# A graph attention loop on one core: operands of long VectorE instructions moved to PSUM, and one matmul in place of two

## The reference, cut to what matters

```
for t in range(3):
    xw = x @ W[t];  a_s = xw @ att_src[t];  a_d = xw @ att_dst[t]
    e_raw  = leaky_relu(a_s[src] + a_d[dst], 0.2)
    m      = maximum(segment_max(where(edge_type == t, e_raw, -inf), dst), e_self)
    w_edge = where(edge_type == t, exp(e_raw - m[dst]), 0)
    num    = segment_sum(w_edge[:, None] * xw[src], dst) + w_self[:, None] * xw
    denom  = segment_sum(w_edge, dst) + w_self
    out   += num / denom[:, None] + bias[t]
```

## Time and profile before

| | us |
|---|---|
| median of 3 timed runs | 4762.41 |
| lowest and highest of them | 4758.4, 4772.9 |
| span of the profiled execution | 4747.3 |
| TensorE busy in it | 4230.1 (89%) |
| VectorE busy in it | 2606.6 (55%) |
| ScalarE busy in it | 1243.8 (26%) |
| POOL busy in it | 3328.1 (70%) |

### The profile page before, as it was taken

One profiled execution on the slowest core, in us unless ns is written; L12 is line 12 of the kernel. 1 busy time (PEld: TensorE's weight loads), 2 busy tenths in 40 slices (PEclk: granted clock), 3 DMA queues, 4 the chain that ended last, 5 costly groups with the idle time before them and its releaser, 6 DMA issues. The chain is left out here.

```text
span 4747.3 us, 64017 instructions
## 1 busy us (share of the span) xinstructions
PE 4230.1 (89%) x18574; PEld 3279.7 (69%) x18575; DVE 2606.6 (55%) x6278; ACT 1243.8 (26%) x3966; POOL 3328.1 (70%) x3261
## 2 busy tenths in 40 slices
PE   7899999999999999999977888888989988898988
PEld 5677777777777777777755667776767766676776
DVE  6777777777777777777755222233322332333233
ACT  4433333333333333333322111111111111111111
POOL 3777777777777777777712777777777777777774
PEclk9655566666666666666657666666566566656567
DMA  2222222222222222222233222222222222222223
GB/s 80 50 50 47 48 48 48 48 48 48 48 48 48 48 48 48 48 48 48 48 70 97 72 70 70 70 72 70 70 71 70 71 70 71 69 71 70 70 70 73
DMA packets 215746, 288.25 MB, mean 61 GB/s; under 512 B 136193, under 2 KB 143929, under 8 KB 215722
## 3 DMA queue, kind: packets, MB, share of 16 engines
q0 software_dynamic: 105472, 222.39, 20.0%
q1 hardware_dynamic: 110250, 65.57, 5.0%
HBM read 277.81 MB, written 9.81 MB: 61 GB/s over the span
## 5 line engine op out<-in xcount | busy, mean ns | idle before, releaser
L54 POOL DMA_INDIRECT ae_xg<-table,ae_idx x1620 | 1675.0, 1034 | 639.7 <-issue 464.0
L54 POOL DMA_INDIRECT ce_xg<-table,ce_idx x1620 | 1623.2, 1002 | 499.9 <-issue 493.6
L1041 DVE TENSOR_TENSOR ce_msg<-ce_ps_f,ce_fb 128x768 f32<-128x768 f32 x270 | 258.6, 958 | 1359.9 <-PE ce_ps_f L995 1359.9
L1014 PE MATMUL ce_ps_h<-ce_ea,ce_fw 50*128 50x384 f32 x1080 | 664.2, 757 | 248.5 <-DMA ce_ea<-in_edge_attr 246.8
L995 PEld LDWEIGHTS ce_ps_f<-ce_fw,ce_hid 128*128 128x128 f32 x3240 | 657.7, 307 | 247.6 <-issue 247.6
L551 PE MATMUL ae_ps_a<-ae_e,ae_xg 128*128 128x96 f32 x3240 | 768.9, 401 | 64.4 <-DVE ae_e L662 64.4
L551 PEld LDWEIGHTS ae_ps_a<-ae_e,ae_xg 128*128 128x128 f32 x3240 | 648.8, 292 | 165.2 <-DVE ae_e L662 89.7
L975 ACT ACTIVATE ce_hid<-ce_ps_h,ce_fb 128x768 f32<-128x768 f32 x270 | 243.3, 901 | 1871.2 <-PE ce_ps_h L1014 1871.2
L995 PE MATMUL ce_ps_f<-ce_fw,ce_hid 128*128 128x128 f32 x3240 | 733.1, 411 | 0.0
L512 ACT ACTIVATE ae_e<-ae_e,ae_sc 128x96 f32<-128x96 f32 x1620 | 459.7, 362 | 955.3 <-DVE ae_e L654 955.3
L1004 PEld LDWEIGHTS ce_ps_a<-ce_hot,ce_msg 128*128 128x128 f32 x3240 | 591.7, 278 | 0.0
(11 more groups left out here) (141 smaller groups left out, 3634.1 us busy)
## 6 DMA issues: line engine op xcount, KB each, us to landing
ce_ea<-in_edge_attr SPq DMA_DIRECT2D x270, 150.0 KB
ae_xg<-table,ae_idx POOLq DMA_INDIRECT x1620, 2.6
ce_xg<-table,ce_idx POOLq DMA_INDIRECT x1620, 2.6
fa_inv_den<-rden SPq DMA_DIRECT2D x7, 1344.0 KB, 7.5
ae_idx<-in_src SPq DMA_DIRECT2D x276, 3.0 KB
...
```

Of the source, the lines that this page charges most:

```text
L54: eng.indirect_dma_start(out=out, out_offset=None, in_=table[:, :], in_offset=bass.IndirectOffsetOnAxis(ap=idx, axis=0)).then_inc(done, 16)
L1014: last = nc.tensor.matmul(ps_h[:, k * 512:k * 512 + H], fw1[:, :], ea[:, s % XS, k * H:(k + 1) * H], start=True, stop=True)
L1041: nc.vector.tensor_tensor(msg[:, s % 3, :, :], ps_f[s % 2][:, 0:CH * D].rearrange("p (c f) -> p c f", c=CH), fb2[:, :].unsqueeze(1).to_bro ...
```

## The change

All of it is in the attention loop.

- `iota` (0 to 95) is copied once into a PSUM bank, `ps_held`, and `off` reads it there. A new part of `look_up`, `hold`, copies the unit's scores (128x6) into the same bank, and `mask` reads them there.
- ScalarE writes the exponentials into two PSUM banks, `ps_e`, not double buffered, three chunks in each; `weights` reads them there and writes the SBUF tile as before, as two instructions of 288 columns instead of one of 576. `off` stays in SBUF.
- For that banks are shared anew: the transpose and `ps_z` share one, and the rise (now `fall`), the denominators and the sums of a unit share `ps_a`. The exponential of the rise stays in PSUM, in place, and `scale_sums` and `scale_denominators` read it there. Since the sums are written to the same bank, both are moved ahead of `weights`.
- The constant matrix has SLOPE in row 0 and -1 in row 32. One matmul over 64 rows of the state takes SLOPE * a_d minus the maximum straight from it, in place of L568 and L579. It waits for `s_max`, since it reads the maximum that the fourth part of `raise_max` writes, and stands behind the matmul of the fall.

```
+    c[0, 2 * P:3 * P] = SLOPE
     c[32, 2 * P:3 * P] = -1
...
+        ps_tz, ps_held = pb("ps_tz"), pb("ps_held")
+        ps_c, ps_a, ps_e = ([pb(f"ps_{k}{b}") for b in range(2)] for k in "cae")
...
-                        nc.scalar.activation(by_chunk[b][:, c, :], by_chunk[b][:, c, :], ACT.Exp, bias=sc2[:, b, c:c + 1])
+                        nc.scalar.activation(ps_e[c // 3][:, c % 3 * KEYS:(c % 3 + 1) * KEYS], by_chunk[b][:, c, :], ACT.Exp, bias=sc2[:, b, c:c + 1])
...
-                    nc.scalar.activation(rescale[:, b, :], ps_d[b][:, KEYS:2 * KEYS], ACT.Exp).then_inc(s_e, 1)
+                    nc.scalar.activation(ps_a[b][:, 2 * KEYS:3 * KEYS], ps_a[b][:, 2 * KEYS:3 * KEYS], ACT.Exp).then_inc(s_e, 1)
...
-                        nc.tensor.matmul(kv(ps_c[b][:, KEYS:2 * KEYS]), h.slope[0:1, :], state[0:1, :, bass.ds(base[s], W)], start=True, stop=False).then_inc(s_dst, 1)
...
                         pe.wait_ge(s_rise, n)
-                        nc.tensor.matmul(ps_c[b][:, KEYS:2 * KEYS], h.less_row32[0:64, :], rise[:, 0, :], start=False, stop=True).then_inc(s_c, 1)
-                        nc.tensor.matmul(ps_d[b][:, KEYS:2 * KEYS], h.less_row32[0:64, :], rise[:, 1, :], start=True, stop=True).then_inc(s_fall, 1)
+                        pe.wait_ge(s_max, n)
+                        nc.tensor.matmul(ps_a[b][:, 2 * KEYS:3 * KEYS], h.lower[0:64, :], fall[:, :], start=True, stop=True).then_inc(s_fall, 1)
+                        nc.tensor.matmul(kv(ps_c[b][:, KEYS:2 * KEYS]), h.lower[0:64, :], state[0:64, :, bass.ds(base[s], W)], start=True, stop=True).then_inc(s_c, 1)
...
-                        nc.vector.tensor_tensor(off[:, s % 3, :, :], h.iota.unsqueeze(1).to_broadcast([P, CH, KEYS]),
+                        nc.vector.tensor_tensor(off[:, s % 3, :, :], held_iota.unsqueeze(1).to_broadcast([P, CH, KEYS]),
...
+                    elif part == "hold":
+                        dve.wait_ge(s_score, n)
+                        nc.vector.tensor_copy(held_sc[:, b, :], sc[:, b, :]).then_inc(s_held, 1)
...
-                                                   in1=sc[:, s % 2, :].unsqueeze(2).to_broadcast([P, CH, KEYS]), op0=ALU.mult, op1=ALU.add).then_inc(s_masked, 1)
+                                                   in1=held_sc[:, s % 2, :].unsqueeze(2).to_broadcast([P, CH, KEYS]), op0=ALU.mult, op1=ALU.add).then_inc(s_masked, 1)
...
+                    for k in range(2):
+                        part = slice(k * CH // 2, (k + 1) * CH // 2)
+                        last = nc.vector.scalar_tensor_tensor(out=by_chunk[b][:, part, :], in0=off[:, s % 3, part, :], scalar=0.0,
+                                                              in1=ps_e[k][:, 0:CH // 2 * KEYS].rearrange("p (c k) -> p c k", k=KEYS),
+                                                              op0=ALU.is_equal, op1=ALU.min)
+                    last.then_inc(s_wgt, 1)
...
                     if weigh:
+                        scale_sums(n - 2, s - 2, base(2), fresh and s == 2)
+                        scale_denominators(n - 2, s - 2, base(2), fresh and s == 2)
                         weights(n - 2, s - 2)
                     if look:
                         look_up(n, s, i, unit, "pick")
                     if chain:
                         raise_max(n - 1, base(1), 0, fresh and s == 1)
-                    if weigh:
-                        scale_sums(n - 2, s - 2, base(2), fresh and s == 2)
+                    if look:
+                        look_up(n, s, i, unit, "score")
                     if chain:
                         raise_max(n - 1, base(1), 1, False)
                     if look:
-                        look_up(n, s, i, unit, "score")
+                        look_up(n, s, i, unit, "hold")
                     if chain:
                         raise_max(n - 1, base(1), 2, False)
-                    if weigh:
-                        scale_denominators(n - 2, s - 2, base(2), fresh and s == 2)
+                    if look:
+                        look_up(n, s, i, unit, "twice")
                     if chain:
                         raise_max(n - 1, base(1), 3, False)
-                    if look:
-                        look_up(n, s, i, unit, "twice")
```

More of the change, by code:

```diff
@@ L466, in attention_edges @@
         high, high_k = sb("high", [P, KEYS]), sb("high_k", [KEYS, 1])
-        top, rise = sb("top", [64, KEYS]), sb("rise", [64, 2, KEYS])
-        rescale = sb("rescale", [P, 2, KEYS])
-        ps_t, ps_z = pb("ps_t"), pb("ps_z")
-        ps_c, ps_a, ps_d = ([pb(f"ps_{k}{b}") for b in range(2)] for k in "cad")
+        top, new, fall = sb("top", [64, KEYS]), sb("new", [64, KEYS]), sb("fall", [64, KEYS])
+        ps_tz, ps_held = pb("ps_tz"), pb("ps_held")
+        ps_c, ps_a, ps_e = ([pb(f"ps_{k}{b}") for b in range(2)] for k in "cae")
+        ps_z = ps_tz[:, P:P + KEYS]
+        held_iota = ps_held[:, 0:KEYS]
+        held_sc = ps_held[:, KEYS:KEYS + 2 * CH].rearrange("p (b c) -> p b c", b=2)
         idx_in = [sem(f"idx_in{s}") for s in range(SL)]
@@ L474, in attention_edges @@
             sem(k) for k in "landed xg_free pool_turn steps key_ready begun rise_zero".split())
-        (s_oh, s_pick, s_score, s_off, s_masked, s_high, s_turned, s_highk, s_z, s_top, s_new, s_rise, s_max,
+        (s_oh, s_pick, s_score, s_held, s_off, s_masked, s_high, s_turned, s_highk, s_z, s_top, s_new, s_rise, s_max,
          s_dst, s_c, s_pre, s_sub, s_e, s_wgt, s_sum, s_scaled, s_dscaled, s_acc, s_den, s_fall) = (sem("s_" + k) for k in (
-             "oh pick score off masked high turned highk z top new rise max dst c pre sub e wgt sum scaled dscaled acc den fall").split())
-        row_ps, row_out, row_max, merged, den_out = (sem(k) for k in "row_ps row_out row_max merged den_out".split())
-        row_banks = ps_a, ps_c, ps_d
+             "oh pick score held off masked high turned highk z top new rise max dst c pre sub e wgt sum scaled dscaled acc den fall").split())
+        row_ps, row_out, row_max, merged, den_out, iota_held = (sem(k) for k in "row_ps row_out row_max merged den_out iota_held".split())
+        row_banks = ps_a, ps_c, ps_e
         block = ctx.enter_context(nc.Block())
@@ L519, in turn @@
                         if not (first and s < 1):
-                            exps(n - 1, (s - 1) % SL)
+                            exps(n - 1, (s - 1) % SL, first and s < 2)
                         if not (first and s < 2):
@@ L554, in sums @@
                         for c in range(CH):
-                            last = nc.tensor.matmul(ps_d[b][64:65, 0:KEYS], h.ones[:, 0:1], by_chunk[b][:, c, :], start=(c == 0), stop=(c == CH - 1))
+                            last = nc.tensor.matmul(ps_a[b][64:65, KEYS:2 * KEYS], h.ones[:, 0:1], by_chunk[b][:, c, :], start=(c == 0), stop=(c == CH - 1))
                         last.then_inc(s_sum, 1)
@@ L564, in turn @@
                         pe.wait_ge(s_high, n)
-                        nc.tensor.transpose(ps_t[0:KEYS, 0:P], high[:, :], h.ident).then_inc(s_turned, 1)
-                        nc.tensor.matmul(kv(ps_c[b][:, 0:KEYS]), h.ones[0:1, :], state[0:1, :, bass.ds(base[s], W)], start=True, stop=True)
-                        nc.tensor.matmul(kv(ps_c[b][:, KEYS:2 * KEYS]), h.slope[0:1, :], state[0:1, :, bass.ds(base[s], W)], start=True, stop=False).then_inc(s_dst, 1)
+                        nc.tensor.transpose(ps_tz[0:KEYS, 0:P], high[:, :], h.ident).then_inc(s_turned, 1)
+                        nc.tensor.matmul(kv(ps_c[b][:, 0:KEYS]), h.ones[0:1, :], state[0:1, :, bass.ds(base[s], W)], start=True, stop=True).then_inc(s_dst, 1)
                         pe.wait_ge(s_highk, n)
@@ L627, in highest_key @@
                     dve.wait_ge(s_turned, n)
-                    nc.vector.tensor_reduce(out=high_k[:, :], in_=ps_t[0:KEYS, 0:P], op=ALU.max, axis=AX.X).then_inc(s_highk, 1)
+                    nc.vector.tensor_reduce(out=high_k[:, :], in_=ps_tz[0:KEYS, 0:P], op=ALU.max, axis=AX.X).then_inc(s_highk, 1)
                 def raise_max(n, base, part, fresh):
@@ L636, in raise_max @@
                         dve.wait_ge(s_z, n)
-                        nc.vector.tensor_tensor(kv(top[32:33, :]), kv(ps_z[32:33, 0:KEYS]), m, ALU.max).then_inc(s_top, 1)
+                        nc.vector.tensor_tensor(kv(top[32:33, :]), kv(ps_z[32:33, :]), m, ALU.max).then_inc(s_top, 1)
                     elif part == 1:
                         dve.wait_ge(s_top, n)
-                        nc.vector.scalar_tensor_tensor(out=rise[32:33, 0, :], in0=ps_z[32:33, 0:KEYS], scalar=SLOPE, in1=top[32:33, :],
+                        nc.vector.scalar_tensor_tensor(out=new[32:33, :], in0=ps_z[32:33, :], scalar=SLOPE, in1=top[32:33, :],
                                                        op0=ALU.mult, op1=ALU.max).then_inc(s_new, 1)
@@ L643, in raise_max @@
                         dve.wait_ge(s_new, n)
```

(4 more changed lines are left out.)

24 lines of the change are left out of this document (13 added, 11 removed).

## The result

The changed kernel takes 4993.06 us (median of 4 runs, 4986.69 to 5001.1) against 4764.61 us (4 runs, 4758.4 to 4772.9) on the same chip: ratio 1.0481, 95% interval [1.0464, 1.0498]. It is 228 us slower. A second session gave 4992.05 against 4765.52, ratio 1.0478 [1.0454, 1.0501]. The forecast was 4943, so its sign and mechanism came true and 50 us were missing.

A forecast was written before the change was run, and what follows sets the result against it. TensorE was taken as full, VectorE's chain level with it at L579. Step 9.34 less 0.14 is 9.20, 0.67 more; 270 x 0.67 = 181 us on 4747 gives 4928, with 15 us 4943; range 4865 to 5000.

The forecast's parts named there:

- sign and mechanism: Attention loop: slower, because VectorE's longer chain makes TensorE wait for weights and maximum; slower by over 0.3% given 0.86.
- the sums at 2.90: TensorE's first half of the sums (L551), forecast to start about 2.91 us behind the transpose, waiting for the weights.
- the pair at 4.79: TensorE's matmuls L584 and L585, forecast to start 4.80 us behind the transpose instead of 4.23, waiting for `raise_max` part 3.
- behind it: TensorE from the pair's start to the next transpose: taken as unchanged, 4.54 us.
- `less_max` waits: VectorE at `less_max` waits for L585, losing some 0.65 us, hidden ahead of the transpose.
- The hold copy: VectorE's copy of the scores into PSUM: taken at 0.20 us, possible 0.08 to 0.28.
- a held VectorE instruction: Moved `scale_sums` on VectorE, held by an input in another quadrant; without the hold the step would be 0.11 us shorter.
- the 15 us: Added to the forecast time, as the amount by which the median lies over the profile's span.
- the return of the full-speed stretch: Time the 2.4 GHz stretches give back: 0.32 us a step before, forecast 0.14 after, bounds 0 and 0.32.
- the much slower case: Rival: clock stays at 0.50 and L584/L585 cost more; step 9.4 to 9.55, 4997 to 5037 us; chance 0.08.
- TensorE's own work as the bound: Rival: losing L568 stays a gain, 0.5 a step, 135 us, 4627; chance 0.09 together with the POOL rival.
- POOL as the pacer: Rival: gathers held up by VectorE pace the step; 135 us faster, about 4630; chance 0.09 together with TensorE's rival.

The follow-up runs named there:

- e4: Changed kernel with the rise's factors in SBUF again and both scalings behind part 3 of `raise_max`; ratio 1.0208 to the kernel before, disturbed session.
- e5: The kernel of e4 again, in another disturbed session; ratio 1.0334 to the kernel before.
- e11: The kernel of e4 again, in an undisturbed session; 4836.78 us against 4760.59 for the kernel before, ratio 1.0151.
- e7: Changed kernel with the fall matmul waiting only for the rise, the maximum's wait moved ahead of the pair's second matmul; ratio 1.0171 to the kernel before, disturbed session.
- e2_ahead: Kernel before with only the two scalings moved ahead of the weights; ratio 1.0254 to the kernel before, disturbed session.
- e12: Kernel before with merged matmul, its wait apart, weights right behind `highest_key`, scalings behind `raise_max`, operands in SBUF; 4655.6 us against 4760.59, ratio 0.978.
- e6: Kernel before with only the merged matmul, which waits for `s_max` ahead of the pair; ratio 0.9748 to the kernel before, disturbed session.
- e1: Kernel before with only the iota operand of `off` in PSUM, transpose and `ps_z` sharing a bank; ratio 1.0027 to the kernel before, disturbed session.

## Why the prediction was right, and where its size was off

**The steps that held.** The working was one step at 1.2 GHz, and it came out row by row: the sums at 2.90 (predicted 2.91), the pair at 4.79 (4.80), the step at 9.39 (9.34). The missing 0.05 is what I called "behind it": 4.54 us, read from a step whose last tenth of a microsecond lay at full speed already (the transpose at 1225.30 takes 0.32); at 1.2 GHz it is 9.39 - 4.79 = 4.60. TensorE's saved 0.56 us turned into the wait for the weights. Both causes are shown apart: taking the scalings out of the chain takes the sums from 2.90 to 2.33 and the pair to 4.23 to 4.30 (e4, e5, e11), and parting the waits takes the pair from 4.79 to 4.43 (e7). `less_max` waits 96.8 / 160 = 0.60 where it waits (predicted 0.65), and as said the transposes do not feel it. The hold copy costs 0.20 as taken, and the two halves of the weights take 0.82 together, the 0.37 and 0.45 of the working. Gathers at 0.945 were foretold at 0.95, POOL's longer wait too. The transpose's wait on L634 is gone (in one step of six its weight load still waits 0.3 us), where it was 0.46. The extra 0.03 of a held VectorE instruction appears as worked out, L609 to L684 in 0.21 us; in e2_ahead, where the same scaling reads its factors from SBUF, it starts 0.09 behind the instruction for the types (1099.98 and 1100.07). Here the rule of the Trainium skill ("VectorE: DVE Perf Modes", Two Vector instructions with no wait between them) and the trace agree.

**Readings that were wrong beside the sum.** I took 1.74 us from the sums to the pair as TensorE's own time, from one step. It is 1.53 (e2, e7, e12); in the earlier trace rows the rest is a wait that the profile does not mark there, but does in other steps of the kernel before (TensorE in order of time):

```profile
1235.92 1.59 PE L551 MATMUL ae_ps_a<-ae_e,ae_xg 128*128 128x96 f32 x6
1237.76 0.71 PE L579 MATMUL ae_ps_c<-ae_rise,cst 64*128 64x96 f32 x2 [0.24 <-DVE ae_rise L644]
```

VectorE's chain was thus not level with TensorE but 0.2 us behind it. The forecast did not hang on it, since the maximum at 4.80 came later than either (4.65 or 4.44), but the expectations for e2 and e7 did, and missed by about that: e7 was to bring 0.14 to 0.25 and brought 0.33. I also named only L644 among TensorE's waits of before and called TensorE full; L662's 49.9 us were overlooked. In every second step, the one that begins at full speed, VectorE's chain already decided the kernel before. And the 15 us that I added for what lies around the span are only the distance between a quick execution and the median.

**The term that was mis-sized.** It is the return of the full-speed stretch. I took 0.14 us a step, with bounds of 0 and 0.32. Measured: 0.02, a mean step of 9.37 beside 9.39 at 1.2 GHz. I had counted the end of the denominators and the transpose as shorter. In the step shown the stretch begins with the transpose, so the denominators gain nothing, and the 0.13 of the transpose bring the sums to 2.77 instead of 2.90; behind them VectorE's chain decides, the pair stands at 4.77 and the step takes 9.36. In addition the full-speed stretches became rarer, 0.56 granted instead of 0.60. This term is 0.12 x 270 = 32 us. The step at 1.2 GHz, 9.39 for 9.34, is another 14 us. Together they are 46 us, and the loop grew by 226 us where 181 was said. The last 4 or 5 us up to 4993 are within the spread of single runs. The forecast of the time was kept by its width: 4993 lies 7 us under the upper end of the range, and 4 us under the rival of the much slower case.

**Where the 228 us lie.** After against e11_back, that is the scalings ahead of the weights with their factors in PSUM: 4993 - 4837 = 156 us, 0.53 a step in the mean. E11_back has them behind the whole of `raise_max`, where before had one of them ahead of the rise, so this is the price of their place in the changed kernel and not of undoing one edit. E11_back against before: 76 us, 0.31 a step, and none of it in a step at 1.2 GHz (8.90 and 8.91). This second part is the return of the full-speed stretch, 0.37 before and 0.05 in e11. E6_merged, which has nothing of the change but the merged matmul, shows the same: in its steps with full speed the pair stands at 4.08 to 4.31, never at before's 3.53, because it waits for the end of `raise_max`. That the operands in PSUM, the halves and the copy add nothing to this part is not shown. So the loss has two parts: one is VectorE's order, which lengthens every step; the other, by the rows of e6 and e11, is the late wait for the maximum, which, once the scalings are out of the way, lengthens only the steps that full speed would have shortened. E11_back with the two waits parted was not run. Behind the loop nothing is changed: the spans differ by 252 in one pair of profiles and 244 in the other, and the loop has 226 of it in both. The rest, 26 and 18, is more than the medians leave (228 - 226); the two profiles of before are of quick executions.

**The rivals.** TensorE's own work as the bound asked for an L584 before 4.23; it stood at 4.79. But e12 shows that such a gain is there once the order allows it: 0.38 a step in the mean, where the rival said 0.5. POOL as the pacer fell in e1 and by its waits. The much slower case nearly came true: the granted clock is lower, at 0.56 though and not at 0.50, and the step of 9.37 lies just under its 9.4.
